# A Mamba block and a mixture-of-experts layer on one core: the opening stages merged, the last stage's first chunk made by pairs

## The chip, the cores and the metric

One core of a Trainium2 chip runs the whole kernel in one launch. The metric is the device time of that launch in microseconds (us). The kernel before was timed in three runs: 4453.03, 4454.98 and 4458.05 us, median 4454.98.

## What is computed

The input x has 2 x 4096 tokens of 512 channels, all fp32. With `ln` for a layer norm without weights:

```python
# first half: a Mamba block on ln(x); Di = 1024 channels, N = 16 states
xn = layernorm(ln(x)) * ln_gamma + ln_beta
xz = xn @ W_in.T                                   # 2048 channels: x part and z part
xs = silu(causal_conv4(xz[:, :Di]) + conv_b)
xp = xs @ W_xproj.T                                # 33: 1, B (16), C (16)
dt = softplus(xp @ W_dt.T + b_dt) + 0.001
A  = -exp(A_log);  dA = exp(A * dt)
h  = clip(dA * h + (1 - dA) / (A + 1e-8) * B * xs, -10, 10)     # a scan over the tokens
y  = (sum_n C * h + D_param * xs) * silu(z)
x1 = x + y @ W_out.T
# second half on xf = ln(x1): a gate and two 512 x 512 products
out = x1 + xf @ W_shared.T + bias + w * (xf @ W_expert.T)       # w from the softmax of xf @ W_gate
```

## The kernel before

The 8192 tokens are 16 chunks of 512 tokens (`CH`), the 1024 inner channels 8 blocks `m` of 128 partitions. The kernel is four blocks of engine programs that run one after the other; a block begins only when every engine has ended the one before. Within a block each engine runs its own list in program order, and semaphores (`wait_ge`, `then_inc`) order the engines. Products are made to fp32 accuracy by splitting each operand into an upper part (rounded to fp32r by ScalarE) and a lower part (the rest, by a subtraction), with three matmuls for each tile.

**setup** (L79 to L173). SyncE clears the first columns of some DRAM scratch tensors (L100 to L108) and the four tensors `band_d` of 1 MB each (L111, L112). VectorE derives from A_log the inverse `inv` (L157), the limits `margin` and `an`, and makes for each m a 1.1 MB tile `w` (L166 to L172): 16 diagonal 128 x 128 matrices with `inv` on the diagonal, the transposed inverse, and the small columns (-exp(A_log), D, 10 an). SyncE stores each tile to `w_d[m]` (L116), with two buffers.

**front** (L176 to L742). SyncE loads x, then W_in in two halves of 2 MB, three copies of W_dt and W_xproj, and five small vectors (L288 to L302). All of them but x count on one semaphore, and ScalarE, TensorE and VectorE wait for all 13 (L426, L540, L668). VectorE makes the layer norm statistics and normalizes x (L592 to L606), TensorE turns it (L522), ScalarE scales it into `xnt` and `xnt_hi` (L378), GpSimd makes `xnt_lo` (L353). ScalarE makes the upper part of W_in in two instructions (L430), VectorE the lower part in two (L672). Then come 16 chunks of the same order: TensorE makes 8 blocks of x and 8 of z (L499, 12 matmuls each), with the turning of xs (L510), the rows xp (L530, L566) and dt (L537) in between; VectorE the convolution (L618 to L626), the statistics of the next chunk (L592) after the second convolution, the maximum of xs (L706) and the copy and split of xp (L710, L713). SyncE's list for one chunk (L306 to L328) is written out by hand: 8 stores of xs, 8 of zs, 16 of the turned xs, 2 of dt, the rows, the 16 copies of C (`c_d`, L277), B, and late in the chunk, behind all but the last stores, the load of x for the chunk after next (L326). All of them go through one queue in that order.

**scan** (L745 to L1135). 16 chunks x 8 blocks x 16 states: TensorE makes `ps_d` from `xk` and the band matrix `dm` (L1032), ScalarE moves it (L976) and makes exp (L987), VectorE scans (L1105), GpSimd multiplies two states at a time by C (L965), TensorE sums over the states with the diagonal weights `w_s` (L1045). TensorE's list has `make_d` of the next block and `sum_state` in turns. GpSimd needs the rows of C, which `load_c` brings in pairs. The lists begin with: fill `band_d[0]` from `bt_d` (L817), load the small columns (L871), load `xk`, wait for the fill, load `dm` (L823). Further on SyncE issues this:

```python
for b in range(BATCH):
    gather_ahead(b)                    # L891: DRAM to DRAM, 128 values of 4 bytes
sp.wait_ge(s_ba, 16 * BATCH)           # L893
load_ahead(0)
load_prev(0)
for blk in range(BLOCKS):              # m == 0: load_c(ch, 4) to load_c(ch, 7), L906
```

**ffn** (L1138 to L1633). For each chunk `weigh` (L1437) makes a weighted row product, `self_term` (L1547) multiplies by xs, two more instructions add y and multiply by zs (L1577, L1580 on VectorE for chunk 0, L1313, L1316 on GpSimd for the others), ScalarE makes the upper part of y in one instruction over all 8 blocks (L1375), GpSimd the lower part in four (L1324), and TensorE projects by W_out: for each of four token tiles i, `project(ch, i, h)` is 12 matmuls over the channels of half h (L1427). `residual` (L1556, L1558) adds x and makes statistics. For chunk 0 all of y must be ready (`s_yl`, L1444) and both halves of W_out (`s_lo` 3, L1472) before the first `project`; after each i come two `weigh` of chunk 1. Before its loop TensorE waits for the split of all six weights (L1478). The weights come over ScalarE's queue, the rest over SyncE's; xs and zs of chunk 0 come one block at a time through rings of 4 and 2 slots (L1213, L1221).

Of the kernel before, what the change touches and what calls it, by code (L numbers as in the profile page):

```python
# [4 lines left out]
P = 128  # L5
# [19 lines left out]
W_DIAG, W_INVT = 0, NS * P  # L25
W_BIG = NS * P + P
S_A, S_D, S_LIM = 0, NS, NS + 1
W_SMALL = 2 * NS + 1
W_COLS = W_BIG + W_SMALL

# [13 lines left out]
def build(nc, t_in, out):  # L44
    with ExitStack() as ctx:
# [11 lines left out]
        w_d = nc.dram_tensor("w_d", [MD, P, W_COLS], F32).ap()  # L57
# [5 lines left out]
        ba_d = nc.dram_tensor("ba_d", [BATCH, NCH, NS], F32).ap()  # L63

# [3 lines left out]
        clips = sb("clips", [1, 1], I32)  # L68
        with ExitStack() as early:
# [4 lines left out]
            front(nc, sb, sem, t_in, ident, ones, minus_half, margin, within, clips, xs_d, dt_d, zs_d, xp_d, xt_d, bt_d, c_d)  # L74
        scan(nc, sb, sem, ident, clips, xs_d, dt_d, xp_d, xt_d, bt_d, band_d, c_d, w_d, y_d, ba_d)
        ffn(nc, sb, sem, t_in, ident, minus_half, xs_d, zs_d, xp_d, w_d, y_d, out)


def setup(nc, sb, sem, t_in, ident, ones, minus_half, margin, within, xs_d, xp_d, xt_d, bt_d, band_d, w_d):  # L79
    with ExitStack() as c:  # L80
        zeros = sb("zeros", [P, BAND], c=c)
        a_log = sb("a_log", [P, MD, NS], c=c)
        ea = sb("ea", [P, MD, NS], c=c)
        ap_ = sb("ap_", [P, MD, NS], c=c)
        an = sb("an", [P, MD, NS], c=c)
        inv = sb("inv", [P, MD, NS], c=c)
        d_par = sb("d_par", [P, MD], c=c)
        w = sb("w", [P, 2, W_COLS], c=c)
        ps = c.enter_context(nc.psum_tensor("ps_setup", [NS, MD, P], F32))
        s_in, s_pool, s_exp, s_dve = sem("su_in", c), sem("su_pool", c), sem("su_exp", c), sem("su_dve", c)  # L90
        s_tr, s_w, s_zero = sem("su_tr", c), sem("su_w", c), sem("su_zero", c)
        s_wo = [sem(f"su_wo{i}", c) for i in range(2)]

        with nc.Block() as block:
            @block.sync
            def _(sp):
                sp.dma_start(a_log[:, :, :], t_in["A_log"].rearrange("(m p) n -> p m n", p=P)).then_inc(s_in, 16)
                sp.dma_start(d_par[:, :], t_in["D_param"]).then_inc(s_in, 16)
                sp.wait_ge(s_pool, 1)
                for b in range(BATCH):  # L100
                    sp.dma_start(xs_d[b, :, :, 0:1].rearrange("m p o -> p m o"), zeros[:, 0:MD],
                                 allow_slow_non_contiguous=True).then_inc(s_zero, 16)
                    sp.dma_start(xp_d[b, :, 0:1], zeros[0:NX, 0:1],
                                 allow_slow_non_contiguous=True).then_inc(s_zero, 16)
                    for h in range(2):
                        sp.dma_start(xt_d[h, b, 0:1, :].rearrange("o (p f) -> p (o f)", p=P),
                                     zeros[:, 0:MD]).then_inc(s_zero, 16)
                        sp.dma_start(bt_d[h, b, 0:1, :], zeros[0:1, 0:2 * NS]).then_inc(s_zero, 16)  # L108
# [8 lines left out]
                for i in range(2):  # L117
                    sp.wait_ge(s_wo[i], 16 * MD // 2)
# [1543 lines left out]
```

## Time and profile before

| | us |
|---|---|
| median of the three runs | 4454.98 |
| the profiled execution, its own time | 4454.84 |
| its span, first to last instruction | 4453.1 |
| TensorE busy | 4166.3 (94%) |
| VectorE busy | 3676.1 (83%) |
| ScalarE busy | 3171.4 (71%) |
| GpSimd busy | 3138.2 (70%) |
| mean granted clock of TensorE | 0.981 of full speed |

The engines of the profile are PE (TensorE matmul), PEld (its weight load), DVE (VectorE), ACT (ScalarE), POOL (GpSimd) and SP (SyncE); SPq is SyncE issuing a DMA. Times are counted from the start of the span. The busy shares are means over four stages that have different limits, so the rows further down go by stage.

### The profile page before, as it was taken

The numbers are of one execution on the slowest core, as the hardware profiler recorded it, in microseconds if no ns is written. First come the engines' busy times: TensorE is split into PE (matmuls) and PEld (weight loads), VectorE is DVE, ScalarE is ACT, GpSimd is POOL, SyncE is SP. The second block draws the span as 40 slices with busy tenths as digits, with TensorE's granted clock in tenths as the row PEclk, the third lists the DMA queues.
The fourth block names the chain that finished last, engine by engine and source line by source line (L and its number), as shares of the span: only waits on it lengthen the run. The fifth ranks groups of instructions, "written<-read, shape, count | busy, mean of one in ns | idle before, by whom it ended". The sixth has DMA issues, their size and how long they took to land. (4 is left out here: it accounts for less than half of the span.)

```text
span 4453.1 us, 48998 instructions
## 1 busy us (share of the span) xinstructions
PE 4166.3 (94%) x14186; PEld 2461.5 (55%) x14186; DVE 3676.1 (83%) x4321; ACT 3171.4 (71%) x5821; POOL 3138.2 (70%) x1550
## 2 busy tenths in 40 slices
PE   2999999995999999999999999999999759999999
PEld 1777777774444444444444444444444238888887
DVE  5888888884899999999999999999999744444443
ACT  1666666664899999999999999999999611211111
POOL 0111111110899999999999999999999767777772
PEclk9999999997999999999999999999999879999999
DMA  5566566666576576656665766576656445555550
GB/s 187 190 203 207 186 208 212 214 205 196 152 191 189 155 184 185 184 155 186 187 181 156 193 186 172 158 197 188 168 168 181 142 157 162 169 163 175 176 166 30
DMA packets 581176, 786.71 MB, mean 177 GB/s; under 512 B 102800, under 2 KB 305936, under 8 KB 579368
## 3 DMA queue, kind: packets, MB, share of 16 engines
q1 hardware_dynamic: 570344, 762.57, 58.4%
q10 hardware_dynamic: 10560, 20.97, 1.3%
q8 instruction: 114, 1.87, 0.2%
q14 instruction: 158, 1.29, 0.1%
HBM read 540.17 MB, written 245.18 MB: 176 GB/s over the span
## 5 line engine op out<-in xcount | busy, mean ns | idle before, releaser
L965 POOL TENSOR_TENSOR q<-g,cc 128x1024 f32<-128x1024 f32 x1024 | 2394.6, 2371 | 139.7 <-DVE g L1105 120.6
L1105 DVE TENSOR_TENSOR_SCAN g<-dd,carry,ps_a 128x512 f32<-128x512 f32 x2048 | 2400.3, 1253 | 40.2 <-ACT ps_a L987 24.5
L1045 PE MATMUL ps_y<-q,w_s 128*128 128x512 f32 x4096 | 2098.4, 593 | 24.4 <-POOL q L965 12.7
L987 ACT ACTIVATE ps_a<-dt_s,small 128x512 f32<-128x512 f32 x2048 | 1501.7, 733 | 5.4 <-DVE g L1105 5.4
L976 ACT ACTIVATE dd<-ps_d 128x512 f32<-128x512 f32 x2048 | 1287.7, 629 | 74.7 <-PE ps_d L1032 51.7
L1032 PE MATMUL ps_d<-dm,xk 99*128 99x512 f32 x2048 | 1119.1, 547 | 63.7 <-ACT dd L976 25.9
L1032 PEld LDWEIGHTS ps_d<-dm,xk 99*128 99x128 f32 x2048 | 384.0, 188 | 1223.0 <-ACT dd L976 957.7
L1045 PEld LDWEIGHTS ps_y<-q,w_s 128*128 128x128 f32 x4096 | 778.6, 191 | 184.7 <-issue 59.3
L353 POOL TENSOR_TENSOR xnt_lo<-xnt_f,xnt_hi 128x512 fp32r<-128x512 f32 x64 | 112.5, 1758 | 557.1 <-ACT xnt_hi L378 557.1
L499 PE MATMUL ps_r_f<-xnt_hi,w_hi 128*128 128x512 f32 x1024 | 418.5, 409 | 13.8 <-DVE w_lo L672 13.8
L499 PE MATMUL ps_r_f<-xnt_lo,w_hi 128*128 128x512 f32 x1024 | 402.9, 393 | 0.0
L499 PE MATMUL ps_r_f<-xnt_hi,w_lo 128*128 128x512 f32 x1024 | 401.7, 392 | 0.0
L624 DVE SCALAR_TENSOR_TENSOR conv<-xz,taps,conv 128x512 f32<-128x512 f32 x384 | 288.7, 752 | 13.6
L1313 POOL TENSOR_TENSOR y_c<-y_c,xs_c 128x512 f32<-128x512 f32 x120 | 154.7, 1289 | 128.7 <-DVE xs_c L1547 128.0
L1427 PE MATMUL ps_c<-wo_hi,y_hi 128*128 128x512 f32 x512 | 206.9, 404 | 27.5 <-POOL y_lo L1324 27.5
L346 POOL TENSOR_TENSOR rstd_f<-spread_f,minus_half 128x4 f32<-128x4 f32 x16 | 16.1, 1009 | 306.5 <-DVE spread_f L598 306.5
L499 PEld LDWEIGHTS ps_r_f<-xnt_hi,w_hi 128*128 128x128 f32 x1024 | 193.0, 188 | 62.3 <-DVE w_lo L672 14.2
L499 PEld LDWEIGHTS ps_r_f<-xnt_hi,w_lo 128*128 128x128 f32 x1024 | 193.2, 189 | 48.1 <-issue 7.7
L499 PEld LDWEIGHTS ps_r_f<-xnt_lo,w_hi 128*128 128x128 f32 x1024 | 192.8, 188 | 41.7
L1406 ACT ACTIVATE t_hi<-ps_t_c 128x512 fp32r<-128x512 f32 x64 | 34.9, 596 | 251.1 <-PE ps_t_c L1459 251.1
L1427 PE MATMUL ps_c<-wo_lo,y_hi 128*128 128x512 f32 x512 | 204.9, 400 | 0.0
L1427 PE MATMUL ps_c<-wo_hi,y_lo 128*128 128x512 f32 x512 | 204.6, 400 | 0.0
(162 smaller groups left out, 4439.5 us busy)
## 6 DMA issues: line engine op xcount, KB each, us to landing
w_s<-w_d SPq DMA_DIRECT2D x256, 512.0 KB, 3.8
xk<-xt_d SPq DMA_DIRECT2D x768, 132.0 KB
xt_d<-xt_f SPq DMA_DIRECT2D x256, 256.0 KB, 3.1
cc<-c_d SPq DMA_DIRECT2D x128, 512.0 KB, 11.3
dm<-band_d SPq DMA_DIRECT2D x192, 264.0 KB
xs_d<-xs_f SPq DMA_DIRECT2D x128, 256.0 KB, 2.5
zs_d<-zs_f SPq DMA_DIRECT2D x128, 256.0 KB, 3.0
dt_d<-lg_f SPq DMA_DIRECT2D x32, 1024.0 KB, 6.5
```

Source lines behind the costliest of these rows:

```text
L353: pool.tensor_tensor(xnt_lo[:, ch % 2, q, :], xnt[:, q % 2, :], xnt_hi[:, ch % 2, q, :].bitcast(F32), ALU.subtract).then_inc(s_xl, 1)
L499: last = pe.matmul(ps_r[:, at_bank[kind, m] % RING, :], wp[:, q, cols], xp_[:, ch % 2, q, :], start=(q + j == 0), stop=(q == KD - 1 and j ...
L624: dve.scalar_tensor_tensor(acc, cur[:, j:j + CH], taps[:, m, j:j + 1], acc, ALU.mult, ALU.add).then_inc(s_cv, 1)
L965: pool.tensor_tensor(q[:, s % QB:s % QB + 2, :], g[:, s % GB:s % GB + 2, :], rows, ALU.mult).then_inc(s_q, 2)
L976: act.activation(dd[:, blk % 2, :, BLK * i:BLK * i + BLK], ps_d[:, i % 2, :].rearrange("p (t n) -> p n t", n=NS), ACT.Copy).then_inc(s_dd, 1)
L987: act.activation(ps_a[:, s % AB, :], dt[:, blk % DTB, :], ACT.Exp, scale=small[:, blk % MD, S_A + n:S_A + n + 1]).then_inc(s_a, 1)
L1032: pe.matmul(ps_d[:, i % 2, :], xk[:, (2 * blk + i // HALF) % XB, i % HALF, :], dm[:, i, :, :].rearrange("p t n -> p (t n)"), start=True, s ...
L1045: pe.matmul(ps_y[:, blk % 2, :], w[:, half % WB, at:at + P], q[:, s % QB, :], start=(n == 0), stop=(n == NS - 1)).then_inc(s_n, 1)
L1105: dve.tensor_tensor_scan(g[:, s % GB, :], dd[:, m % 2, n, :], ps_a[:, s % AB, :], carry[:, m, n:n + 1], ALU.add, ALU.mult).then_inc(s_g, 1)
L1313: pool.tensor_tensor(y[:, m, :], y[:, m, :], xs[:, m % XRING, :], ALU.add).then_inc(s_add, 1)
L1406: act.activation(t_hi[:, :, i, :], ps_t[:, i % 2, :].rearrange("p (k t) -> p k t", t=P), ACT.Copy).then_inc(s_te, 1)
L1427: last = pe.matmul(dst, a(j), b(j), start=(j + p == 0), stop=(j == total - 1 and p == 2))
```

## The change

Three places change; the arithmetic stays the same.

**Opening.** `setup` is gone. `front` loads x first, then A_log, gamma and beta, then W_in in four pieces of 1 MB with a semaphore each; the rest follows. ScalarE and VectorE split W_in piece by piece between the four `xnt` tiles, and TensorE waits for piece q only before its matmuls of q. The values from A_log are made by VectorE after that (8 small instructions); the small columns stay on the chip. The diagonal tiles are no longer made on the chip and stored: zeros are stored to DRAM, in pieces of 512 bytes, two stores of 0.5 MB for each of the chunks 0 to 7, and 2048 values of 4 bytes are stored onto each diagonal one chunk later. The four band tensors are cleared in chunks 8 to 11 (pieces of 528 bytes), the first band is filled in chunk 12. One of each chunk's new stores, and the diagonal, stand in SyncE's list ahead of the load of x.

**Scan.** The fill, the load of the small columns, their waits and `gather_ahead` with its wait are gone from its list; the gathers stand at the end of `front`, where SyncE waits for them.

**Last stage.** For chunk 0 xs, y and zs come in pairs of blocks (three DMAs of 0.5 MB), the weights over SyncE's queue between them; VectorE makes the lower part of y; TensorE projects half 0 of each tile between the last four `weigh` of chunk 0.

```diff
-            setup(nc, sb, sem, t_in, ident, ones, minus_half, margin, within, xs_d, xp_d, xt_d, bt_d, band_d, w_d)
@@ front, SyncE
+                def clear_band(i):
+                    e, h = i // 2, i % 2
+                    sp.dma_start(band_d[e, h, 0:1, :].rearrange("o (j n) -> o j n", n=ZEROS),
+                                 bcast(zeros[0:1, 0:1], [(0, BAND // ZEROS), (1, ZEROS)])).then_inc(s_zero, 16)
+                    sp.dma_start(band_d[e, h, 1:CH + 1, :].rearrange("(p s) n -> p (s n)", p=P).rearrange("p (j n) -> p j n", n=ZEROS),
+                                 bcast(zeros[:, 0:1], [(0, SUB * BAND // ZEROS), (1, ZEROS)])).then_inc(s_zero, 16)
+                def clear_diagonal(m, h):
+                    sp.dma_start(w_d[m, :, bass.ts(h, NS * P // 2)].rearrange("p (n k) -> p n k", k=P),
+                                 bcast(zeros[:, 0:1], [(0, NS // 2), (1, P)])).then_inc(s_zero, 16)
+                def fill_diagonal(m):
+                    whole = w_d[m, :, :]
+                    sp.dma_start(bass.AP(tensor=whole.tensor, offset=whole.offset, ap=[(W_PITCH + 1, P), (P, NS)]), inv[:, m, :],
+                                 allow_slow_non_contiguous=True).then_inc(s_diag, 16)
...
                 load_x(0)
+                for dst, src in ((a_log, t_in["A_log"].rearrange("(m p) n -> p m n", p=P)),
+                                 (gamma[:, :], t_in["ln_gamma"]), (beta[:, :], t_in["ln_beta"])):
+                    sp.dma_start(dst, src).then_inc(s_gb, 16)
+                for k in range(KD):
+                    sp.dma_start(raw_win[k], t_in["W_inT"][k * P:(k + 1) * P, :]).then_inc(s_wq[k], 16)
...
+                load_x(1)
+                sp.wait_ge(s_pool, 1)
+                clear_edges()
...
                     store_turned(ch, 5)
                     store_b(ch)
+                    if 0 < ch <= MD:
+                        sp.wait_ge(s_zero, 16 * (EDGES + 2 * ch))
+                        fill_diagonal(ch - 1)
+                    if ch < MD:
+                        clear_diagonal(ch, 0)
+                    elif ch < MD + 4:
+                        clear_band(ch - MD)
+                    elif ch == MD + 4:
+                        sp.wait_ge(s_bto, 32)
+                        sp.wait_ge(s_zero, 16 * (EDGES + 2 * MD + 8))
+                        fill_first_band()
                     store_zs(ch, 6)
                     store_turned(ch, 6)
                     load_x(ch + 2)
                     store_zs(ch, 7)
                     store_turned(ch, 7)
+                    if ch < MD:
+                        clear_diagonal(ch, 1)
...
                 sp.wait_ge(s_xpo, CHUNKS * 32)
+                for b in range(BATCH):
+                    gather_ahead(b)
+                sp.wait_ge(s_diag, 16 * (4 + MD + 2 + BATCH))
@@ front, ScalarE
-                act.wait_ge(s_wt, 13 * 16)
-                for q in range(KD):
-                    scale_xnt(0, q)
-                for j, stage in enumerate((v, lg)):
...
+                act.wait_ge(s_gb, 48)
+                act.activation(ea, a_log, ACT.Exp).then_inc(s_ea, 1)
+                upper_win(0)
+                scale_xnt(0, 0)
+                scale_xnt(0, 1)
+                upper_win(1)
+                scale_xnt(0, 2)
+                scale_xnt(0, 3)
+                upper_win(2)
+                upper_win(3)
+                act.wait_ge(s_wt, 9 * 16)
@@ front, TensorE
+                            if ch == 0:
+                                pe.wait_ge(s_lo, q + 1)
...
+                        if ch == 0 and m == 3:
+                            turn_inverse()         # 8 transposes of 128 x 16
@@ scan, SyncE
-                fill_band(0)
-                sp.dma_start(small[:, :, :], w_d[:, :, W_BIG:W_COLS].rearrange("m p s -> p m s"),
-                             allow_slow_non_contiguous=True).then_inc(s_sm, 16)
                 load_x(0, 0)
-                sp.wait_ge(s_band, 32)
...
-                for b in range(BATCH):
-                    gather_ahead(b)
-                sp.wait_ge(s_ba, 16 * BATCH)
@@ ffn, SyncE
+                            sp.dma_start(dst, bass.AP(tensor=src.tensor, offset=src.offset,
+                                                      ap=[(0, 4), (PAD, NS), (1, CH)])).then_inc(s_rows, 16)
...
                 load_rows(0)
+                sp.dma_start(raw_inv, invt_d).then_inc(s_wt[0], 16)
                 sp.dma_start(d_par[:, :], t_in["D_param"]).then_inc(s_dp, 16)
+                load_pair(0)
+                load_pair(1)
+                load_weights(1, "W_outT", 0)
+                load_pair(2)
+                load_pair(3)
+                load_weights(2, "W_outT", HALF * P)
                 load_x(0)
@@ ffn, TensorE
                 pe.wait_ge(s_lo, 1)
-                for m in range(MD):
+                pe.wait_ge(s_set, 4)
+                for m in range(HALF):
                     weigh(0, m)
+                for i in range(SUB):
+                    weigh(0, HALF + i)
+                    if i == 0:
+                        pe.wait_ge(s_lo, 2)
+                    project(0, i, 0)               # i == 0 waits for s_yl: the lower parts of 4 channel blocks
                 pe.wait_ge(s_lo, 3)
                 for i in range(SUB):
-                    project(0, i, 0)
                     project(0, i, 1)
@@ ffn, VectorE
                 for m in range(MD):
                     if m % 2 == 0:
-                        dve.wait_ge(s_y[m // 2], 16)
+                        dve.wait_ge(s_y[m // 2], 48)
+                    if m == HALF:
+                        lower_weights(1)
...
+                    if m in (2, 4, 6):
+                        lower_first(m // 2 - 1)
+                lower_first(YL - 1)
+                for j in range(2, len(parts)):
                     lower_weights(j)
```

## Rows read from the trace of the kernel before

**Rows 1.** Busy time by stage: start:end, length, busy us by engine, clock, DMA share, GB/s.

```profile
0.00:93.80 93.80, 6.33 (x24) 3.81 (x24) 44.07 (x63) 15.34 (x13) 7.60 (x15) 1.00 0.58 209
93.80:1056.00 962.20, 955.26 (x4304) 731.34 (x4304) 822.77 (x1424) 611.21 (x882) 122.58 (x75) 1.00 0.61 200
1108.00:3534.00 2426.00, 2363.27 (x6128) 1048.61 (x6128) 2400.47 (x2049) 2363.91 (x4720) 2394.65 (x1024) 0.99 0.64 174
3534.00:3652.00 118.00, 39.16 (x120) 27.05 (x120) 46.61 (x55) 19.88 (x15) 53.89 (x35) 0.62 0.57 183
3652.00:4453.00 801.00, 792.13 (x3592) 646.36 (x3592) 354.99 (x720) 140.19 (x168) 559.43 (x402) 1.00 0.47 151
```

**Rows 2.** Timeline, the opening: start, duration, engine, line, [idle before <- releaser].

```profile
0.74 0.45 SPq L97 DMA_DIRECT2D a_log<-in_A_log  x1
...
48.75 0.38 SPq L244 DMA_DIRECT2D x_f<-in_x  x1
...
54.70 2.47 DVE L592 BATCH_NORM_STATS2 stats_f<-x_f 128x6 f32<-128x512 f32 x4 [10.71 <-DMA x_f<-in_x]
...
58.80 1.92 DVE L606 TENSOR_SCALAR x_f<-x_f,mv_f,rstd_f 128x512 f32<-128x512 f32 x4 [1.15 <-POOL rstd_f L346]
...
72.07 0.78 ACT L378 ACTIVATE xnt_f<-ps_t_f,beta,gamma 128x512 f32<-128x512 f32 x1 [68.36 <-PE ps_t_f L522]
...
81.38 3.61 ACT L430 ACTIVATE w_hi<-v_f 128x4096 fp32r<-128x4096 f32 x1
...
93.83 0.80 PE L499 MATMUL ps_r_f<-xnt_hi,w_hi 128*128 128x512 f32 x1 [13.84 <-DVE w_lo L672]
...
98.98 0.60 ACT L386 ACTIVATE xz<-ps_r_f 128x512 f32<-128x512 f32 x1 [9.54 <-PE ps_r_f L499]
```

**Rows 3.** Busy time by stretch: 4-byte stores, large loads, loads of short pieces.

```profile
5.30:6.00 0.70, 0.31 (x2) 0.26 (x3) 0.47 (x2) 0.00 (x0) 0.00 (x0) 1.00 0.68 6
50.00:60.00 10.00, 0.00 (x0) 0.00 (x0) 4.12 (x12) 0.00 (x0) 1.03 (x1) 1.00 1.00 386
1078.00:1086.00 8.00, 0.00 (x0) 0.00 (x0) 0.17 (x1) 0.00 (x0) 0.00 (x0) 0.50 0.70 204
```

**Rows 4.** Timeline, one chunk of the front, from its load of x on.

```profile
338.35 0.45 SPq L244 DMA_DIRECT2D x_f<-in_x  x1
...
346.26 2.47 DVE L592 BATCH_NORM_STATS2 stats_f<-x_f 128x6 f32<-128x512 f32 x4 [1.00 <-DMA x_f<-in_x]
...
377.02 0.69 DVE L633 TENSOR_TENSOR xt_f<-ps_t_f,xt_f 128x512 fp32r<-128x512 f32 x1 [1.07 <-ACT xt_f L369]
...
383.36 0.68 DVE L713 TENSOR_TENSOR xp_f<-xp_f 33x512 fp32r<-33x512 f32 x1 [0.73 <-ACT xp_f L460]
...
384.17 0.43 PE L566 MATMUL ps_xp<-ident,xp_f 33*128 33x33 f32 x4
```

**Rows 5.** Timeline, the start of the scan.

```profile
1074.40 1.54 SPq L817 DMA_DIRECT2D band_d<-bt_d  x2
...
1078.34 3.08 SPq L823 DMA_DIRECT2D dm<-band_d  x6
...
1111.02 1.70 SPq L856 DMA_DIRECT2D ba_d<-xp_d  x2
...
1127.72 2.48 SPq L847 DMA_DIRECT2D cc<-c_d  x4
...
1135.54 30.22 POOL L965 TENSOR_TENSOR q<-g,cc 128x1024 f32<-128x1024 f32 x13 [12.32 <-DMA cc<-c_d]
```

**Rows 6.** Timeline, the first chunk of the last stage.

```profile
3556.85 0.75 DVE L1547 SCALAR_TENSOR_TENSOR xs_c<-ps_b,d_par_c,xs_c 128x512 f32<-128x512 f32 x1 [7.96 <-DMA y_c<-y_d]
...
3577.24 4.49 DVE L1531 TENSOR_TENSOR wo_lo<-o_c,wo_hi 128x2048 fp32r<-128x2048 f32 x2
...
3595.53 0.76 PE L1427 MATMUL ps_c<-wo_hi,y_hi 128*128 128x512 f32 x1 [20.92 <-POOL y_lo L1324]
...
3652.14 0.80 PE L1427 MATMUL ps_c<-wo_hi,y_hi 128*128 128x512 f32 x1 [6.61 <-POOL y_lo L1324]
```

More of the change, by code:

```diff
@@ L176, in front @@
-def front(nc, sb, sem, t_in, ident, ones, minus_half, margin, within, clips, xs_d, dt_d, zs_d, xp_d, xt_d, bt_d, c_d):
+            front(nc, sb, sem, t_in, ident, ones, minus_half, margin, within, clips, small, xs_d, dt_d, zs_d, xp_d, xt_d, bt_d, c_d,
+                  band_d, w_d, invt_d, ba_d)
+        scan(nc, sb, sem, clips, small, xs_d, dt_d, xt_d, bt_d, band_d, c_d, w_d, y_d, ba_d)
+        ffn(nc, sb, sem, t_in, ident, minus_half, xs_d, zs_d, xp_d, invt_d, y_d, out)
+def front(nc, sb, sem, t_in, ident, ones, minus_half, margin, within, clips, small, xs_d, dt_d, zs_d, xp_d, xt_d, bt_d, c_d,
+          band_d, w_d, invt_d, ba_d):
@@ L310, in _ @@
                     store_xs(ch, 3)
+                    if ch == 0:
+                        sp.wait_ge(s_ivt, 1)
+                        for r in range(3):
+                            sp.dma_start(invt_d[NS * r:NS * (r + 1), :, :].rearrange("n m p -> n (m p)"), raw_invt).then_inc(s_diag, 16)
+                        sp.dma_start(invt_d[3 * NS:4 * NS, :, :], bcast(zeros[0:NS, 0:1], [(0, MD), (1, P)])).then_inc(s_diag, 16)
                     store_zs(ch, 0)
@@ L331, in _ @@
                 sp.wait_ge(s_xpo, CHUNKS * 32)
+                for b in range(BATCH):
+                    gather_ahead(b)
+                sp.wait_ge(s_diag, 16 * (4 + MD + 2 + BATCH))
                 sp.wait_ge(s_dto, CHUNKS * 32)
@@ L742, in _, with scan @@
                 dve.wait_ge(s_fl, 3)
-def scan(nc, sb, sem, ident, clips, xs_d, dt_d, xp_d, xt_d, bt_d, band_d, c_d, w_d, y_d, ba_d):
+def scan(nc, sb, sem, clips, small, xs_d, dt_d, xt_d, bt_d, band_d, c_d, w_d, y_d, ba_d):
     STEPS = MD * NS
@@ L778, in scan @@
         S = lambda n: sem("s_" + n, c)
-        s_sm, s_band, s_ba = S("small"), S("band"), S("ba")
+        s_band, s_ba = S("band"), S("ba")
         s_dm = [S(f"dm{i}") for i in range(PIECES)]
@@ L1182, in ffn @@
         YL = MD // 2
[L1184 to L1186 removed]
+        raw_inv = xn[0:ROWS, 0:2, :].rearrange("p s (m t) -> p (s m) t", t=P)
+        blank = x[ROWS:P, 1, 1:4, :].rearrange("p s (m t) -> p (s m) t", t=P)
+        raw_g = x[:, 1, 0, :].rearrange("p (k t) -> p k t", t=P)
+        parts = ((raw_inv, inv[0:ROWS, :, :], None),
                  (o[:, 0, :, :], wo_hi[:, 0:HALF, :], wo_lo[:, 0:HALF, :]),
@@ L1190, in ffn @@
                  (raw_g, wg_hi[:, :, :], wg_lo[:, :, :]))
+        xs0 = [xs[:, m, :] if m < XRING else y_lo[:, m, :].bitcast(F32) for m in range(MD)]
+        xs0_pairs = [xs[:, 0:2, :], xs[:, 2:4, :], y_lo[:, 4:6, :].bitcast(F32), y_lo[:, 6:8, :].bitcast(F32)]
+        zs0_pairs = [t[:, k:k + 2, :, :].rearrange("p k s t -> p k (s t)").bitcast(F32) for t in (t_hi, t_lo) for k in (0, 2)]
         def rows(tensor, ch):
```

360 lines of the change are left out of this document (155 added, 205 removed).

## The prediction

> **What bounds the kernel now.** I read the busy time by stage first [rows 1], then the timeline where a stage begins or ends. The reader should see three stages that one engine fills, and three gaps. In the front TensorE is busy 955.3 of 962.2 us, so nothing that only frees another engine helps there. In the scan GpSimd is busy 2394.7 of 2426.0, and in the last stage's loop TensorE 792.1 of 801.0. The gaps are the first 93.8 us, in which TensorE works 6.3; the 52 us between front and scan; and the 118 us before the last stage's loop, TensorE 39.2 of them at a mean clock of 0.62. The change works on the gaps, but puts DMA work from the first of them into the front. The sum is made against the profiled execution's 4454.84, which is the median (4454.98) within 0.2; 0.2% is 9 us, about what a measurement of this kernel can tell from no change.
>
> **The opening.** Before, SyncE loads x only at 48.75, because setup runs until then; the first product of W_in starts at 93.83 and its result is read at 98.98 [rows 2]. After, the load of x can stand where A_log's stands now, at 0.7. The path from there, in durations of [rows 2]:
> - x is issued 5.95 before the statistics start, and the norm ends (58.80 + 1.92) 11.97 after the issue: 12.7.
> - Four turns and four pairs of scalings: from 72.07 to 81.38 there are four pairs and three turns, 9.31; a fourth turn makes it 10.5. The copy of W_in piece 1 (half of 3.61, so 1.8) stands between them and hides behind a turn in part: net 1.0. Last scaling ends at 24.2.
> - Pieces 2 and 3 are copied: 27.8. VectorE's subtraction for 128x2048 takes 2.25 (4.49 for two in [rows 6]); those of pieces 2 and 3 run from 26.0 to 30.5.
> - W_in itself is no limit: x and W_in are 5.2 MB, 13.6 us at the 386 GB/s of [rows 3], so all is there by 18.
> - The last three matmuls of the first block start at 30.5; its result is read at 32.0 instead of 98.98, 67.0 earlier.
>
> Against it: TensorE had 12 matmuls of a cold clock behind it at 98.98 and has only 3 after 30.5, so about 1.3 more is lost, and the 8 small transposes of the inverse cost 1.0 on TensorE. VectorE's small instructions (the copy for W_dt, then eight of 0.2 to 1.0) let the first convolution start 2 us late; chunk 0 has no dt to add, which covers it, and costs 2 to 3 if it does not. Taken: **64.7 gained**, from 62 to 68.
>
> **The DMA work moved into the front.** This is where I choose. SyncE's queue is in order, and its new stores stand ahead of the load of x for the chunk after next. In [rows 4] that load is issued at 338.35 and VectorE waits for it until 346.26: 7.5 us for 1.05 MB that need 2.7 at 386 GB/s, so a backlog is already ahead of it, and VectorE already waits 1.00. What is put in front of x makes it later in full. Behind the statistics VectorE has one wait, 1.07 before L633, and then the maximum, the copy and the split (383.36 + 0.68) lead straight to TensorE's L566 at 384.17. So 1.07 us per chunk are covered, the rest stops TensorE.
>
> The price of the stores in chunks 1 to 7: 0.52 MB of zeros in 512-byte pieces take 1.35 us at the rate of large loads, or 2.6 at 204 GB/s, which the stretch of short pieces shows [rows 3]. The 2048 values of 4 bytes: the 0.70 us of [rows 3] move 4.2 KB of such values, about 1050, so 1.4. Together 2.75 to 4.0; I take 3.4, as no row has 512-byte stores and the nearest are loads. Chunk 8 has a band (1.08 MB, 2.8 to 5.3, taken 4.0) and a diagonal, 5.4; chunks 9 to 11 a band, 4.0. If each stall is the delay less 1.07, they are 7 x 2.3 + 4.3 + 3 x 2.9 = 29. But a stall gives the queue its own length to drain before the next chunk asks for x, so delay and stall settle at half: **14.5 lost**. The ends are 0 (nothing can be gained by more stores) and 39 (4.0, 6.7 and 5.3, without halving). The stores behind the last of a chunk run in the idle part of the queue (DMA share 0.61 [rows 1]); without that cover they would add 1.4 to 2.6 per chunk to the same delay. The Trainium skill, "DMA: Bandwidth & Descriptors", Specifications, gives 512 bytes as the least size at line rate. By it the zeros would cost the lower figure and the loss would be 10, the sum 4365. The short-piece stretch of this trace speaks for more.
>
> **Front's end and the scan.** The two gathers now stand in front of the wait that ends the front, beside the store of 2 MB of dt. Their issue takes 1.70 [rows 5]; I count **1.0 lost** (0 to 3). In the scan, SyncE's list reaches dm 3.94 us after its start, of which three issues of xk stay (1.5, half of dm's six in 3.08): **2.4 gained** (1 to 4). Then the gathers: issued by 1112.72, waited for, and the rows of C for states 8 on go out only at 1127.72; GpSimd, which bounds this stage, waits 12.32 for them [rows 5]. Without it the most that can come is 12.3. What is late next: VectorE must wait at the change to block 1 for ScalarE's last tiles, about one step of GpSimd (30.22 / 13 = 2.3), and the first pair of C lands behind xk and dt (0.65 MB, 1.4 with issue). **8.6 gained** (5 to 12). The rest of the scan is GpSimd's and does not change.
>
> **The last stage's first chunk.** Ahead of pair 0 the queue has rows and inverse, 0.52 MB, and the pair is 1.57: 5.4 us at 386 GB/s. With the 3.2 by which x's first use exceeds its transfer [rows 2], the first product of VectorE is at 3534 + 8.6 = 3542.6 instead of 3556.85. Its list up to the second half of W_out: eight blocks of 2.1 (from 3556.85 to 3577.24 are 8, less 3.5 of waits), four lower parts of y at 1.1 and two of W_out at 2.25, together 25.9. To that come TensorE's projections, which stand in its list ahead of `weigh` 5, 6 and 7: VectorE waits about 6 for the first and 3 for the others. So half 1 starts at 3577.5; before, the first projection started at 3595.53 [rows 6]. From there to the loop's first projection (3652.14) before took 56.6. 48 matmuls fall out of it. They are 5.1 us a dozen at the low clock, 2.8 at the full, but the products between hold their pace, so I count 2.9 for the first tile and 1.7 for each of the others: 8. The loop starts at 3626; **25 gained** after rounding for the clock, from 19 (all of it at the low clock) to 30. GpSimd's y_lo, for which TensorE waited 20.92 before, goes to VectorE in those four lower parts. The Trainium skill's rule on using all 16 engines (same page, Rules for kernel authors) says that an outermost dimension of 4 keeps a DMA to 4 engines. The new row loads have one; two loads of 131 KB at a quarter of 386 GB/s take 2.7 instead of 0.7, and the sum would be 4372. No row here shows it.
>
> **Sum.** 4454.8 - 64.7 + 14.5 + 1.0 - 2.4 - 8.6 - 25 = 4369.6, so 4370. Its own range is 4357 to 4382.
>
> **Rivals.**
> - *The stores hide.* For it: the queue is idle 39% of the front. Against it: the wait of 1.00 in [rows 4], just where it counts. Loss 0: 4355.
> - *No halving.* If the queue has gaps between the stores of dt and x, a stall does not drain it, and 29 to 39 are lost: 4384 to 4394.
> - *The projections hold VectorE up.* `project` of half 0 stands ahead of `weigh`; with the clock low in every one, half 1 starts at 3582 or later, and xs, zs and y of chunk 1 come late as well, so only the earlier start of 14 is kept: 4381.
> - *Slower than before.* One mechanism: the 4-byte stores onto a diagonal, 512 bytes and more apart, cost far more than those of [rows 3]. With 25 us each, x is 26.6 late and TensorE stands (26.6 - 1.07) / 2 = 12.8 in each of chunks 1 to 8, 102 in all, and 5 in the others: 4462. It decides from about 24 us on, 17 times what [rows 3] show; little speaks for it.
>
> **Chances.** Forecast 0.48, hidden 0.20, no halving 0.20, projections 0.10, slower 0.02. The range takes in the first four with the bounds of the opening on both sides: 4348 to 4396. Faster by over 0.2% in all but the last: 0.97; within 0.2%: 0.01; slower 0.02.
>
> **What would show it.** Right: the first result of W_in read near 32; in chunks 1 to 8 VectorE's wait before L592's counterpart of 1 to 3 us, and TensorE idle 1 to 2 before the transposes of xp, nothing of it in chunks 13 to 15; GpSimd's second wait for cc under 2; the last stage's first product near 8.6 after its start, and 92 from its start to the loop's first projection instead of 118. Wrong: waits for x as before (hidden), or TensorE idle over 2 in every one of those chunks (no halving, or dear stores); a wait for cc still near 10, which would mean that the gathers were not what held the list.

## The result, and the profile after

The changed kernel takes 4469.56 us in the median of 17 runs (4458.72 to 4481.17), the kernel before 4455.88 in the median of 17 beside it (4449.62 to 4461.67). The ratio is 1.0031, with an interval of 1.0023 to 1.0039: slower by 0.3%, where 4370 was forecast with 4396 as the upper end. The profiled execution spans 4468.5 us. The views by stage (first of the kernel after, the counterpart of [rows 1]) show that each stage still has its bound, but that two of them grew:

```profile
0.00:30.00 30.00, 8.18 (x25) 5.20 (x25) 13.61 (x17) 15.52 (x15) 8.08 (x15) 0.98 0.84 241
30.00:1056.00 1026.00, 977.93 (x4303) 735.33 (x4303) 837.17 (x1438) 617.89 (x887) 98.55 (x75) 0.98 0.67 201
1104.00:3574.00 2470.00, 2377.12 (x6128) 1062.54 (x6128) 2406.25 (x2049) 2364.97 (x4720) 2399.72 (x1024) 0.98 0.67 171
3574.00:3667.00 93.00, 39.82 (x120) 27.95 (x120) 48.57 (x58) 20.52 (x17) 45.06 (x31) 0.67 0.73 235
3667.00:4468.00 801.00, 792.12 (x3592) 646.46 (x3592) 354.82 (x720) 140.10 (x168) 559.81 (x402) 1.00 0.48 152
```

The columns are those of [rows 1]. TensorE starts its steady work at 30 instead of 94, but its front now holds 48 us of idleness (977.93 of 1026) where it had 7. The scan takes 2470 us for the same 2400 of GpSimd, so GpSimd is idle 70 us where it was idle 31. The gap before the last stage's loop is 93 instead of 118, and the loop is 801 as before.

The borders between the stages, from the timelines, give the ledger that the rest of this text goes by. "Front" counts from the moment the first result of W_in is read to the issue of the last stores of dt; the scan from VectorE's first scan to the start of the last stage.

```
us                                 before     after   difference
first result of W_in read           98.98     32.02     -67.0
front                              968.0    1027.7      +59.7
last dt store to SyncE's next        7.4      12.2       +4.8
from there to the first scan        33.7      32.6       -1.1
scan                              2426.0    2469.8      +43.8
last stage                         919.0     894.2      -24.8
span                              4453.1    4468.5      +15.4
```

**The opening did what was forecast.** In the timeline of the kernel after, x is issued at 0.74, TensorE's last piece starts at 30.36 and the first result is read at 32.02:

```profile
0.74 0.46 SPq L161 DMA_DIRECT2D x_f<-in_x  x1
6.71 2.48 DVE L606 BATCH_NORM_STATS2 stats_f<-x_f 128x6 f32<-128x512 f32 x4 [6.71 <-DMA x_f<-in_x]
30.36 0.77 PE L503 MATMUL ps_r_f<-xnt_hi,w_hi 128*128 128x512 f32 x1 [1.01 <-DVE w_lo L686]
32.02 0.60 ACT L378 ACTIVATE xz<-ps_r_f 128x512 f32<-128x512 f32 x1 [3.58 <-PE ps_r_f L503]
```

**The front waits for x.** The view of the tile x_f on VectorE has one line for this, 15.5 us in 7 waits before (10.7 of them in the opening). After:

```profile
  DMA x_f<-in_x: 56.6, 14
```

All but 6.7 of it, 49.9 us in 13 waits, are in the chunks, where there were 4.8. The queue around one of these waits, first SyncE's issues and then windows of 4 us:

```profile
477.41 0.51 SPq L232 DMA_DIRECT2D w_d<-inv  x1
477.96 1.44 SPq L226 DMA_DIRECT2D w_d<-zeros  x1
481.39 0.65 SPq L161 DMA_DIRECT2D x_f<-in_x  x1
478.00:482.00 4.00, 4.00 (x18) 3.27 (x18) 3.36 (x9) 2.32 (x5) 0.00 (x0) 1.00 1.00 118
482.00:486.00 4.00, 4.00 (x18) 3.19 (x17) 3.39 (x7) 3.99 (x4) 0.00 (x0) 1.00 1.14 117
486.00:490.00 4.00, 4.00 (x19) 3.22 (x18) 2.50 (x5) 3.97 (x4) 0.00 (x0) 1.00 1.05 358
498.00:510.00 12.00, 12.00 (x57) 9.67 (x56) 11.50 (x27) 5.28 (x10) 0.00 (x0) 1.00 0.31 115
```

From 478 to 486 every DMA engine is busy and moves 118 GB/s: these are the 4-byte elements of the diagonal and the zeros, and behind them x. From 498 the queue is nearly empty again. From chunk 1 to chunk 7 the loads of x are issued 65.0 us apart (156.76 to 546.65 for six), where they were 60.4 apart; chunk 8 takes 69.0, chunks 9 to 11 64.0 to 65.6, and chunk 13 is back at 59.6. From the load of x in chunk 0 to the one in chunk 12 it is 778.4 against 723.8: 54.6 us.

**The scan has a wait that it didn't have.** The scan's loop issues the same instructions in the same order as before. The tile view of xk on TensorE, from 1140 to 3520, before and after:

```profile
  ACT dd L976: 23.7, 107
  DMA xk<-xt_d: 6.3, 8
```

```profile
  DMA xk<-xt_d: 51.5, 19
  ACT dd L994: 20.2, 95
```

About once a chunk of 150 us xk is late; TensorE's d, ScalarE's copy and VectorE's scan follow it, and GpSimd stands. Windows of the stretch in which a chunk's dm, cc, xk and w all load at once, before and after, at the same DMA share:

```profile
2020.00:2050.00 30.00, 28.98 (x77) 13.20 (x76) 30.00 (x27) 29.55 (x61) 29.92 (x14) 1.00 0.94 250
```

```profile
2030.00:2060.00 30.00, 26.44 (x63) 12.17 (x62) 26.73 (x24) 24.87 (x50) 26.41 (x13) 0.89 0.95 229
```

The same engines' time moves 8% fewer bytes. The DMA view says so for the whole middle of the scan (1500 to 3000): queue, packets, MB and share, before and after.

```profile
q1 hardware_dynamic: 229515, 266.18, 64.9%
```

```profile
q1 hardware_dynamic: 225388, 261.32, 67.9%
```

What can make the same transfers dearer? A candidate is the tiles' places. The program lays its SBUF tensors one behind another in the order in which they are declared. Before, `small` had 33 columns per block of channels (1056 bytes per partition) and stood in the scan between w_s and dt_s. After, it has 32 columns (1024 bytes), since D left it, and stands ahead of all. So everything from dt_s on moved down by 32 bytes: cc from 36608 to 36576, dm from 77568 to 77536, xk from 110336 to 110304. The three stood at multiples of 256 bytes and now stand 32 short of one. (dt_s, which a DMA writes too, went the other way, from 32 short of a multiple of 256 to 64 short; w_s stands 64 short in both.) That is the theory that the first experiments were made for.

**The last stage did what was forecast, but for its first step**: the loop's first projection is 93.4 us after the stage's start (92 forecast, 118.0 before), and the whole is 24.8 shorter. The first product on VectorE, 11.6 after the start, is 3.0 later than forecast. It waits for TensorE's `weigh`, and that for the rows of B and C, which GpSimd gets late, 6.4 after the start:

```profile
3580.71 1.25 POOL L1335 TENSOR_TENSOR c_r<-b_r,c_r 64x512 f32<-64x512 f32 x1 [2.91 <-DMA c_r<-xp_d]
3577.00:3579.00 2.00, 0.00 (x0) 0.00 (x0) 0.00 (x0) 0.00 (x0) 0.80 (x2) 0.50 0.30 79
```

For two microseconds in which the rows, the inverse and the first pair are all issued or being issued, the DMA share is 0.30, that is 4.8 of 16 engines. Experiment 2 comes back to this.

### The profile page after: what moved, and what is told of

It is laid out like the page before. It is cut to its first block and busy times, and to the rows that moved or that the text cites. A ratio compares the mean times of both kernels' runs of the same rounds, so it can differ in the third digit from the quotient of the medians.

```text
span 4468.5 us, 48879 instructions
## 1 busy us (share of the span) xinstructions
PE 4205.3 (94%) x14186; PEld 2481.8 (56%) x14186; DVE 3665.6 (82%) x4288; ACT 3172.3 (71%) x5825; POOL 3111.2 (70%) x1546
## 5 line engine op out<-in xcount | busy, mean ns | idle before, releaser
L1049 PE MATMUL ps_d<-dm,xk 99*128 99x512 f32 x2048 | 1157.1, 566 | 110.6 <-DMA xk<-xt_d 57.9
L333 POOL TENSOR_TENSOR xnt_lo<-xnt_f,xnt_hi 128x512 fp32r<-128x512 f32 x62 | 86.7, 1399 | 573.7 <-ACT xnt_hi L370 573.7
```

Source lines behind the costliest of these rows:

```text
L333: pool.tensor_tensor(xnt_lo[:, ch % 2, q, :], plain(ch, q), xnt_hi[:, ch % 2, q, :].bitcast(F32), ALU.subtract).then_inc(s_xl, 1)
L1049: pe.matmul(ps_d[:, i % 2, :], xk[:, (2 * blk + i // HALF) % XB, i % HALF, :], dm[:, i, :, :].rearrange("p t n -> p (t n)"), start=True, s ...
```

## Experiments

Stage lengths are read from each run's own timeline, as in the ledger. Kernels are the changed one with an edit, unless said. How far a stage differs between profiles that have it alike: the scan takes 2415.3 to 2420.1 us in the six profiles with dm and xk at multiples of 256, and 2466.8 to 2480.3 in the four of the changed kernel with cc, dm and xk 32 short of one. The front is told below.

**1. The 32 bytes, both ways.** The first:

```diff
         x_prev = sb("x_prev", [P, 2, 1], c=c)
+        pad = sb("pad", [P, 8], c=c)
         cc = sb("cc", [P, CN * CR, CH], c=c)
```

> The changed kernel with one unused tensor of 32 bytes per partition ahead of cc, so that cc, dm, xk, dd, g and q stand at the SBUF addresses that they had in the kernel before (multiples of 64; in the changed kernel they stand 32 bytes off). Theory A (DMAs that write cc, dm and xk at 32 modulo 64 take longer, and xk is then late once a chunk of the scan): the 43.9 us that the scan grew go, first scan to the last stage's start comes back to 2426 (before) or a few us under, the waits of the scan for DMA xk fall from about 58 us to under 10, cc lands in 11.4 us instead of 12.8; total about 4426 (4420 to 4432). Rival B (the scan grew for another reason, such as the order in which its DMAs now meet, or the tensors that the changed opening writes): nothing moves, 4470, the scan stays at 2470. The front is the same under both: 1060 to its last store of dt.

Measured: 4430.05 (4 runs), ratio to before 0.9936 (0.9919 to 0.9952). The scan is 2418.3. The tile view of xk, 1140 to 3520:

```profile
  ACT dd L995: 21.0, 98
  DMA xk<-xt_d: 8.9, 10
```

The same line in the kernel before:

> The kernel before with the same unused 32 bytes ahead of cc: cc, dm, xk and all behind them move to 32 modulo 64, nothing else changes. Theory A: the scan grows from 2426 to about 2470, cc lands in about 12.8 us, waits for DMA xk come up to about 58 us, total about 4499 (4490 to 4505). Rival B: 4455, within 5 us.

Measured: 4515.33, ratio 1.0128 (1.0112 to 1.0145). The scan is 2479.6 where it was 2426.0, 53.6 more; everything else is within 3 us of before (last stage 919.4). So 32 bytes of unused memory cost the kernel before 57 us, and the changed one, with them, comes out 39.5 below its median of 4469.56. Theory A holds in both directions, rival B falls. The first edit changes nothing in the front, yet its profiled front ended at 1072 and not 1060: the changed front's last store of dt is issued at 1059.7 to 1072.1 in six profiles with the same front. In the four profiles that have all new stores behind x it is at 1005.8 to 1007.0. Why the one varies and the other doesn't is not shown.

**2. Which tile.** Four kernels, each in one run, with pads placed so that only some tiles stay off.

Pads ahead of cc and behind xk:

> The changed kernel with 32 unused bytes ahead of cc and again behind xk: cc, dm and xk, which DMAs write, are back at multiples of 64; dd, g, q, carry and y, which the engines write and read, stay 32 off. Theory A1 (the DMAs that write misplaced tiles are the slow ones): first scan to the last stage's start 2418 to 2422, as with all of them moved back. Rival A2 (the engines' or a store's accesses to dd, g, q or y are slowed): stays near 2470.

Measured: scan 2416.8, total 4427.34. What the engines touch (dd, g, q, y) can stand 32 off at no cost.

A pad behind cc alone, and the loads of rows split:

```diff
-                            sp.dma_start(dst, bass.AP(tensor=src.tensor, offset=src.offset,
-                                                      ap=[(0, 4), (PAD, NS), (1, CH)])).then_inc(s_rows, 16)
+                            for r in range(4):
+                                sp.dma_start(dst[NS * r:NS * (r + 1), :], src).then_inc(s_rows, 16)
```

> The changed kernel with 32 unused bytes behind cc: cc alone stays at 32 modulo 64, dm, xk and the rest are at multiples of 64. In the last stage the loads of the rows of B and C go as four DMAs of 16 partitions each instead of one with an outermost dimension of 4. Of the 51.5 us: if the cost goes by bytes written, cc (4.2 MB of the chunk's 26 MB) takes a third at most, and the scan is 2425 to 2435; if xk's rows of 512 bytes carry it, 2418 to 2422; if cc's landing beside the new dm is what makes xk late, 2450 or more. The rows: if a load with an outermost dimension of 4 goes to 4 engines, the last stage's first product is 2 us earlier (9.6 after its start instead of 11.6); if not, it is the same or up to 1 later by its six more issues.

Measured: scan 2415.3. cc's place costs nothing, although it is a DMA that writes it too (in pieces of 4 KB, landing in 11.8 us against 11.3).

The rows, split into four loads each, are there sooner. GpSimd starts on them 5.2 us after the stage's start instead of 6.4, although their issue takes 3.6 instead of 1.2:

```profile
3529.22 1.25 POOL L1336 TENSOR_TENSOR c_r<-b_r,c_r 64x512 f32<-64x512 f32 x1 [1.66 <-DMA c_r<-xp_d]
```

From the end of the last row's issue it is 1.6 us to that, where it was 5.3. So the load with an outermost dimension of 4 was slow by some 3.7 us, the direction of the sentence on 4 engines in the prediction, and the share of 0.30 above fits it; how many engines such a load used, no view shows. The stage gains nothing from it in this form: the pairs behind the rows are issued 2.5 us later, the first product now waits for zs (`[2.67 <-DMA t_hi<-zs_d]`) and comes 12.4 after the start instead of 11.6.

Pads ahead of cc, dm and xk:

> The changed kernel with unused 32 bytes ahead of cc, dm and xk: dm alone stays at 32 modulo 64. By bytes: dm is 3.2 MB a chunk, all of it in the 50 us in which DMA is full, so 2430 to 2440; if dm's writes of 2 KB carry nothing 2418 to 2422.

Measured: scan 2447.1, total 4458.28. The tile view of xk says who waited, and for what, although xk is not the tile at 32:

```profile
  DMA xk<-xt_d: 40.4, 18
```

xk's loads stand behind dm's in the queue, and pay for them. (By these pads xk stood 64 bytes behind a multiple of 256 here.)

Pads ahead of cc and xk and behind xk:

> The changed kernel with xk alone at 32 modulo 64 (cc, dm and all behind xk at multiples of 64). xk is written in pieces of 512 bytes, 6.5 MB a chunk, and is what the scan waits for. If short pieces pay most for the offset, the scan is 2440 to 2465 and w and dt land later between chunks too; if the cost is by bytes, 2430 to 2440.

Measured: scan 2439.1, total 4447.02, waits for xk 28.9 in 16. Against the 2416.8 of the run with all three in place, dm costs 30.3, xk 22.3 and cc nothing. The sum of 52.6 meets the 51.5 to 53 by which the profiled changed kernel is longer than the two with all three in place. That it fits so closely is luck, as each is one run and the scan with all three out of place takes 2466.8 to 2480.3; that dm and xk both cost tens of us, and cc doesn't, is clear of that. dm alone is above the 2430 to 2440 expected by bytes, xk within it.

**3. The front: where the stores stand.**

```diff
                     store_b(ch)
-                    if 0 < ch <= MD:
-                        sp.wait_ge(s_zero, 16 * (EDGES + 2 * ch))
-                        fill_diagonal(ch - 1)
-                    if ch < MD:
-                        clear_diagonal(ch, 0)
...
                     store_zs(ch, 6)
                     store_turned(ch, 6)
                     load_x(ch + 2)
                     store_zs(ch, 7)
                     store_turned(ch, 7)
-                    if ch < MD:
-                        clear_diagonal(ch, 1)
+                    if 0 < ch <= MD:
+                        sp.wait_ge(s_zero, 16 * (EDGES + 2 * ch))
+                        fill_diagonal(ch - 1)
+                    if ch < MD:
+                        clear_diagonal(ch, 0)
+                        clear_diagonal(ch, 1)
...
```

The bands of chunks 8 to 12 move in the same way.

> The changed kernel with the clears and fills of the diagonals and bands issued behind the load of x and the last stores of each chunk instead of ahead of them. Theory F (the chunk's growth is the load of x standing behind the clear and the fill in the queue): the waits before the statistics (49.9 us in 13 times) fall under 10 and the chunk comes back from 65 us to 60 to 61; the front's last store of dt at 1008 to 1020 instead of 1060; total 4418 to 4430. Rival G (the growth is the bandwidth that the clears and fills take, wherever they stand: the stores behind them are as late as x was): the front's end stays within 10 us of 1060 and another wait (for a buffer of zs, xs or xt) takes the place of the one for x; total 4460 or over.

Measured: 4420.60, ratio 0.9912 (0.9896 to 0.9929). The last store of dt is issued at 1006.68, 53.0 earlier, with the same bytes moved. The windows by stage (the front), and the tile view of x_f:

```profile
30.00:1007.00 977.00, 962.28 (x4303) 730.31 (x4303) 829.53 (x1440) 618.88 (x888) 114.86 (x75) 0.99 0.73 211
```

```profile
  DMA x_f<-in_x: 10.3, 5
```

The DMA share is higher than before (0.73), and in the chunks VectorE waits 3.4 us for x in all, where it waited 4.8 before the change. Theory F holds, rival G falls: the stores cost only by standing ahead of x. The scan, which this edit leaves alone, took 2480.3 here, the longest of the four above (xk: 57.4 us in 20 waits), and the profiled execution, 4429.77, is the slowest of the four.

Here the zeros go out with nothing else between them, at 142 GB/s with all engines full:

```profile
469.00:475.00 6.00, 6.00 (x28) 4.81 (x27) 4.72 (x10) 4.55 (x8) 0.00 (x0) 1.00 1.20 142
```

**4. Fills or clears.**

> The changed kernel without the eight fills of the diagonals by 4-byte elements (leaves out: the weights by which the scan sums its states stay zero, so the part of y that comes from them is missing). Theory F1 (most of a chunk's growth of some 5 us is the 2048 elements of 4 bytes): the chunks 1 to 8 come back to about 61 us, the chunks 9 to 12 with their band clears stay near 64; the front's last store of dt near 1030. Rival F2 (the elements cost the 1.4 us of the sum, and the cleared bytes the rest): chunks near 63.5, the last store of dt near 1049.

Measured: 4458.48 in one run, last dt store at 1047.67: the fills cost 12 us by this pair, 1.5 a chunk, but the changed front's own 12 us of variation cover it. The loads of x of chunks 1 to 7 were 62.8 apart instead of 65.0, so by them a fill costs 2.2, and the result is nearer to F2. The next one is cleaner, because with the zeros behind x the front varies little:

> The changed kernel with all clears behind the load of x, and the eight fills of 4-byte elements alone still ahead of it. The fills took about 2.2 us a chunk by the run without them (1047.7 against 1059.7 to 1072.1 at the last store of dt). If a stall is the delay less the cover of 1.07: 8 x 1.1 over the 1007 of the run with everything behind, 1016. If nothing is covered: 1025. If the halving of the prediction held: 1011. The clears then are the rest of the front's loss, about 40 us in 12 chunks.

Measured: 4425.21 in one run, last dt store at 1014.58, 7.9 later than the 1006.68 with everything behind x, 1.0 for each of 8 fills; 1016 was expected with the cover of 1.07 and 1011 with a halving. If 1.07 of the delay are covered and the rest stops TensorE, one fill ahead of x delays it by 2.05. The zeros are the rest: chunks 1 to 7 grew by 4.6, so the whole delay is 5.7 and the 0.52 MB of zeros ahead of x take 3.6, some 146 GB/s, close to the 142 GB/s of the window above. A window of the run without fills has the zeros together with other stores and x:

```profile
466.00:474.00 8.00, 8.00 (x35) 6.30 (x36) 6.49 (x13) 6.12 (x9) 0.00 (x0) 1.00 1.09 184
```

**5. All together.** The pad, the stores behind x, and the two gathers ahead of the last stores of dt:

```diff
+                sp.wait_ge(s_xpo, CHUNKS * 32)
+                for b in range(BATCH):
+                    gather_ahead(b)
                 for h in range(2):
                     store_dt(CHUNKS - 1, h)
-                sp.wait_ge(s_xpo, CHUNKS * 32)
-                for b in range(BATCH):
-                    gather_ahead(b)
```

> The changed kernel with three edits: 32 unused bytes ahead of cc (as in the first experiment), the clears and fills behind the load of x (as in the third), and the two gathers of B issued ahead of the last stores of dt. If the parts add up: last store of dt at 1007, the scan's first load 7.4 instead of 12.2 behind it (1014.5), first scan 31 later, 2418 to the last stage's start (3463), and 894 to 895 for the last stage: 4358 span, 4360 in all, ratio 0.978. If the front's saving came only because the scan was slow (it can't by my reading), or the parts overlap, 4375 or over.

Measured: 4359.95 (5 runs), ratio 0.9785 (0.9772 to 0.9799), which beats both kernels. The windows by stage of its profiled run (4353.0):

```profile
30.00:1007.00 977.00, 962.49 (x4303) 730.52 (x4303) 829.47 (x1440) 619.44 (x888) 114.46 (x75) 1.00 0.71 211
1043.00:3459.00 2416.00, 2363.19 (x6128) 1050.64 (x6128) 2400.41 (x2049) 2365.15 (x4720) 2396.32 (x1026) 1.00 0.63 175
3459.00:3552.00 93.00, 39.85 (x120) 27.95 (x120) 48.66 (x58) 20.52 (x17) 45.21 (x30) 0.67 0.72 235
3552.00:4353.00 801.00, 792.16 (x3592) 646.48 (x3592) 354.83 (x720) 140.17 (x168) 558.49 (x402) 1.00 0.47 152
```

The parts add up: the step from the last dt store to the scan's first load is 7.4, the first scan comes 29.0 later, and the scan is 2415.4.

**6. The last stage's tiles.** There most tiles that loads write stand 32 short of a multiple of 256 in both kernels, y_c and xs_c among them. While their pairs load in the changed kernel, its windows show the queue at full rate:

```profile
3584.00:3590.00 6.00, 2.36 (x3) 0.87 (x3) 3.99 (x6) 0.00 (x0) 0.83 (x1) 0.50 1.05 386
```

A pad there was tried all the same:

> The kernel of the run above with 32 more unused bytes in the last stage behind d_par_c, so that b_r, c_r, xs_c, zs_c, y_c, y_hi, y_lo, x_c and bias, which stand at 32 modulo 64 in the kernel before and in the changed one, come to multiples of 64. Theory A in its general form (any DMA that writes a tile 32 off pays) gives an earlier first product and earlier pairs in the last stage's first chunk: 890 to 893 instead of 895. Against it: the same loads already move 387 GB/s with the offset in the changed kernel, and then nothing changes (within 1 us).

Measured: 4373.95, ratio 0.9811 (0.9798 to 0.9825): 14 us slower than the run above, on the same chip, and the last stage is 909.6 instead of 894.4. Both expectations missed. In the lines of TensorE in the last stage (3560 to 4340), the products with W_shared and W_expert went from 390 to 396 ns each, which is 9 of the 15 us for 1536 of them. First a line of the kernel of experiment 5, then of this one:

```profile
L1455 PE MATMUL ps_c<-ws_hi,t_hi 128*128 128x512 f32 x252 | 98.3, 390 | 0.0
```

```profile
L1456 PE MATMUL ps_c<-ws_hi,t_hi 128*128 128x512 f32 x240 | 95.0, 396 | 0.0
```

The pad had also moved xn_c, t_hi, t_lo, xb_c and o_c to 32 behind a multiple of 64, so a second pad brought them back:

> The last stage of the run before (all aligned from b_r to x_c) came out 15 us longer, 909.6 against 894.4, and the 32 bytes there also moved xn_c, t_hi, t_lo, xb_c and o_c from multiples of 64 to 32 off. Here 32 more bytes ahead of xn_c bring these five back, so that every large tile of the last stage is at a multiple of 64. If it was the place of t_hi and t_lo (the products with W_shared and W_expert took 396 ns each instead of 390, 1536 of them, 9 us), those are back at 390 and the last stage at 894 to 900; and if tiles of loads and of y gain by standing at 64, it is 890 to 893. If it was the tiles from b_r to x_c that lost by being moved, it stays near 910, total 4374.

Measured: 4369.65, ratio 0.9794 (0.9781 to 0.9808), last stage 903.6, the products still at 396. The place of t_hi modulo 64 is not the cause. What is stays open, and a pad in the last stage is no gain: to the loop it is 92.2 here and 95.4 in the run before, against 93.5 without a pad. (This kernel ran on another chip, where the kernel before took 4459.17 instead of 4457.04.)

## Why the prediction was wrong

Against the forecast of 4369.6, the profiled execution took 4470.36, 100.8 more. By terms:

```
term                                     forecast   measured
opening                                    -64.7      -60.3
DMA work ahead of x                        +14.5      +53.0
gathers at the front's end                  +1.0       +4.8
start of the scan's list                    -2.4       -1.1
gathers' wait in the scan                   -8.6       -7.7
places of dm and xk                           0       +51.5
last stage's first chunk                   -25        -24.8
```

The opening is measured by the run with the stores behind x (1006.68 against 1067.01), the DMA work by the difference of that run to the changed kernel (1059.71, the earliest of six; by the others it is up to 65), the gathers' wait by the run with the pad (2418.3 against 2426.0), the places by 2469.8 against 2418.3. No run moved dt_s back, so its part in the -7.7 is not separated.

- *The sentence "The rest of the scan is GpSimd's and does not change" failed*, and with it half of the miss. The diff has no line in that loop, and I took the loop for untouched. But its tiles moved, and TensorE's xk, which [rows 1] can't show as close to late, was: already the kernel before waited 6.3 us for it. No rival had this mechanism. The one that was forecast to end slower (dear 4-byte stores) is not what happened: a fill costs 2.05 of delay, not 25, so that its 4462 lies near the measured time is chance.
- *The halving failed.* I wrote that "a stall gives the queue its own length to drain before the next chunk asks for x". The queue drains in every chunk anyway; a window of the kernel before, shortly after a load of x (457.05), shows it standing still:

```profile
467.00:471.00 4.00, 4.00 (x19) 3.29 (x18) 3.86 (x12) 4.00 (x4) 1.01 (x1) 1.00 0.01 4
```

The backlog ahead of x is made anew in each chunk by the stores issued just before it. No delay is carried over, so no stall can shorten the next one. The numbers agree: the zeros at 142 GB/s are 3.7 us, and with 2.05 for a fill and the cover of 1.07 a chunk grows by 4.7 without a half and by 2.3 with one (2.8 with the dearer fill that a half would imply); 4.6 were measured. And the two prices of a fill, 2.05 from the run with fills alone and 2.2 from the run without them, meet only without a half (with one they would be 3.05 and 4.3). "No halving" was a rival, with a chance of 0.20.

- *The price of the zeros was low.* 3.6 us for 0.52 MB where 2.0 were taken and 2.6 was my upper bound, from a stretch of short loads. Stores of zeros are slower than those loads, 142 GB/s with nothing else in the queue against 204; why is not shown. (A row of w_d is 2209 values, so nearly all of the 512-byte pieces start off a multiple of 64 bytes; no run has them elsewhere.) The fill at 2.05 was 1.4 in the sum. Without the halving my prices would have given 29, and 53 was measured, so the price carries the larger part of the 38.5 that this term is off, the halving 14.5. The first bound, "nothing", was not near. The Trainium skill, "DMA: Bandwidth & Descriptors", Specifications, would have the zeros at line rate, 1.35 us: the run speaks against it still more than the stretch of short loads did.
- *The gathers* stand behind 2 MB of dt in the queue, and the stage waits for their end and not for their issue: 4.8, where I took 1.0 and 3 was the upper end. Issued 8 us earlier, into SyncE's wait for dt, they are free (7.4, as before).
- *The scan's start* is right in size once dm stands in its place: 30.4 from the first load of xk with the pad, 32.6 without. GpSimd's second wait fell from 12.32 to 5.39 and not under 2. In the four runs with dm and xk back in place it is 2.9 to 3.9, so some 2 us of it belong to the places as well. The whole term was still 7.7 of 8.6.
- *The opening* was right in each step; 32.02 is the number forecast. Of its 64.7, 4.4 are missing by the front's end, and the 60.3 lie below my range of 62 to 68. In the run with the stores behind x, chunk 0 is 3.2 longer than before (59.7 from its first result to its load of x, against 56.5), where I had 2.3 for the clock and the transposes; the other 3.3 come in the chunks behind it. Their cause is not shown: that run still has the new stores in its queue, and the tiles of the front from xnt_hi to lg_f stand 32 bytes off their old places modulo 64 as well, which no run tests.
- *The last stage* was right in its total: 93.4 to the loop where 92 was forecast, 24.8 gained where 25 was. The first product came 3.0 late, for the rows; I had named an outermost dimension of 4 as worth 2.0 and left it out of the sum. The second half of the projections started 46.0 after the stage's start instead of 43.5, and from there to the loop it took 47.4 instead of 48.6.

What showed it in the profile: the list at the prediction's end gave waits for x of 1 to 3 us; they are 3.8 in the mean and up to 7.3 (49.9 in 13), which is the sign for "no halving". It had no entry for the scan's loop.

## What to carry to other kernels

A diff that adds, drops or resizes a tile moves every tile behind it, in stages that it doesn't mention. Before you call a stage unchanged, compare the addresses of the tiles that its DMAs write, and keep an unused tile of the difference ready; it is the cheapest experiment there is (32 bytes cost the kernel before 1.3% here). And in a queue that runs in order, background stores belong behind the load that someone waits for, even if the queue is idle 39% of the time: what matters is what stands ahead of that load when it is issued.

## What the runs showed of the hardware

- DMA writes of dm (pieces of 2 KB) and xk (512 bytes) into tiles 32 bytes off multiples of 256 cost the scan 30.3 and 22.3 us in 16 chunks; cc (4 KB) cost nothing at the same offset, and the last stage's loads run at 386 GB/s into tiles 32 short of such a multiple, in both kernels. So the place alone doesn't decide it. Whether the border is 64 or 256 bytes wasn't tried alone; that xk, 64 behind a multiple of 256 in the run for dm, added nothing to the sum speaks weakly for 64, as the sum is of single runs.
- The Trainium skill, "DMA: Bandwidth & Descriptors", How a descriptor splits into AXI transactions, says that a descriptor that starts off a multiple of 256 bytes is fetched in more beats. It says this of reads; here the tiles are written. The direction agrees, 250 to 229 GB/s in the full stretch; no run here shows the mechanism.
- Zeros written to DRAM in pieces of 512 bytes went at 142 GB/s with all DMA engines busy, and 2048 elements of 4 bytes delayed what stood behind them by 2.05 to 2.2 us.
- Two loads of 128 KB with an outermost dimension of 4 were ready 5.3 us after the end of their issue; as eight loads of 16 partitions each, 1.6 us after it.
- Tiles moved by 32 bytes in the last stage made matmuls 396 ns instead of 390, and moving t_hi and t_lo back to multiples of 64 didn't undo it. Not explained.
